# MoE, gates and final layer norm on 28 tiles of 128 tokens instead of 32 batches of 112

## Time and profile before

| what | value |
|---|---|
| median of 3 runs | 868.14 us (867.99 to 869.48) |
| the profiled execution's own time | 868.0 us |
| its span, first to last instruction | 866.2 us |
| PE busy | 829.0 us (96%) |
| DVE busy | 723.7 us (84%) |
| ACT busy | 650.5 us (75%) |

### The profile page before, as it was taken

One profiled execution on the slowest core, in us unless ns is written; L12 is line 12 of the kernel. 1 busy time (PEld: TensorE's weight loads), 2 busy tenths in 40 slices (PEclk: granted clock), 3 DMA queues, 4 the chain that ended last, 5 costly groups with the idle time before them and its releaser, 6 DMA issues.

```text
span 866.2 us, 25528 instructions
## 1 busy us (share of the span) xinstructions
PE 829.0 (96%) x7844; PEld 723.8 (84%) x7844; DVE 723.7 (84%) x2836; ACT 650.5 (75%) x1961; POOL 199.7 (23%) x293
## 2 busy tenths in 40 slices
PE   4789999999999999999999999999999999999985
PEld 3678888888888888888888888888888888888863
DVE  3547888888998888888988898998888998888765
ACT  2458877788887777888877788887777888777760
POOL 2202122222222222222222212222222222222101
PEclk9999999999999999999999999999999999999999
DMA  8634444443434444433444433444444333433300
GB/s 261 163 98 104 114 108 109 123 114 86 104 98 111 109 115 117 95 98 96 113 109 110 123 94 101 100 106 106 113 118 103 99 100 100 108 86 84 92 8 11
DMA packets 89830, 91.08 MB, mean 105 GB/s; under 512 B 19440, under 2 KB 85600, under 8 KB 89696
## 3 DMA queue, kind: packets, MB, share of 16 engines
q1 hardware_dynamic: 89696, 89.45, 41.0%
HBM read 26.84 MB, written 3.67 MB: 35 GB/s over the span
## 4 chain that ended last, share of the span: by engine, by line
PE 87%; DVE 3%; SPq 3%; DMA 2%; issue 2%; ACT 1%; POOL 1%; DVEq 0%; POOLq 0%; ACTq 0%
PE psum L1042 19%; PE psum L920 18%; PE psum L911 11%; PE psum L936 10%; PE psum L986 8%; PE psum L979 7%; PE psum L968 3%; PE psum L1000 3%; SPq L386 2%; SPq L395 1%; PE psum L957 1%; DVE mix L609 1%; PE psum L950 1%; PE psum L962 1%; DMA wout_sb<-in_wout 1%
## 5 line engine op out<-in xcount | busy, mean ns | idle before, releaser
L475 ACT ACTIVATE probs<-masked,nmax 112x375 f32<-112x375 f32 x512 | 312.9, 611 | 77.6 <-DVE nmax L595 76.6
L595 DVE CUSTOM_DVE_ANT_0 masked<-psum,mask_add 112x375 f32<-112x375 f32 x512 | 276.6, 541 | 53.7 <-PE psum L911 42.8
L505 ACT ACTIVATE probsT<-psum 125x336 f32<-125x336 f32 x512 | 228.6, 447 | 63.2 <-PE psum L920 58.3
L920 PE MATMUL psum<-const_sb,probs 112*125 112x112 f32 x1536 | 251.1, 272 | 0.1
L920 PEld LDWEIGHTS psum<-const_sb,probs 112*125 112x125 f32 x1536 | 235.8, 188 | 16.0 <-issue 6.8
L911 PE MATMUL psum<-k_stack,q_stack 96*112 96x376 f32 x512 | 203.4, 397 | 3.3 <-DMA k_stack<-k_hi 2.7
L418 POOL TENSOR_SCALAR var_eps<-moments 112x1 f32<-112x1 f32 x96 | 21.2, 220 | 485.6 <-DVE moments L699 191.1
L609 DVE SCALAR_TENSOR_TENSOR mix<-psum,gate,mix 112x256 f32<-112x256 f32 x224 | 107.7, 481 | 14.6 <-PE psum L1042 1.3
L1042 PE MATMUL psum<-we_hi,x_hi 128*112 128x512 f32 x256 | 108.0, 422 | 2.4 <-DVE mix L609 2.4
L911 PEld LDWEIGHTS psum<-k_stack,q_stack 96*112 96x112 f32 x512 | 90.1, 176 | 22.5 <-issue 13.4
L1042 PE MATMUL psum<-we_hi,x_lo 128*112 128x512 f32 x256 | 100.8, 394 | 0.0
(11 more groups left out here) (110 smaller groups left out, 1438.2 us busy)
## 6 DMA issues: line engine op xcount, KB each, us to landing
k_stack<-k_hi SPq DMA_DIRECT2D x256, 93.8 KB, 2.2
q_stack<-q_hi SPq DMA_DIRECT2D x256, 56.0 KB, 2.0
ctx_sb<-in_context_T SPq DMA_DIRECT2D x32, 376.0 KB, 3.3
k_stack<-k_lo SPq DMA_DIRECT2D x128, 93.8 KB, 2.2
q_stack<-q_lo SPq DMA_DIRECT2D x128, 56.0 KB, 2.0
xT<-in_x_T SPq DMA_DIRECT2D x32, 112.0 KB, 2.2
x_sb<-in_x SPq DMA_DIRECT2D x32, 112.0 KB, 2.2
out_dram<-out_sb SPq DMA_DIRECT2D x32, 112.0 KB, 1.9
```

The lines of the kernel that those rows point to most:

```text
L475: nc.scalar.activation(probs[:, n % RING, :], masked[:, n % RING, :], ACT.Exp, bias=nmax[:, n:n + 1], scale=-1.0, accum_out=probs_sum[a[1] ...
L505: nc.scalar.activation(probsT[:, i % TRING, :], psum[0:KP, T_BANKS[i % 2], 0:KT * TOK], ACT.Copy).then_inc(probsT_copied, 1)
L595: nc.vector.tensor_tensor_reduce(masked[:, n % RING, :], psum[0:TOK, S_BANKS[n % 2], 0:KEYS], mask_add[k][:, :], 1.0, 3.0e38, ALU.add, ALU ...
L920: mm = nc.tensor.transpose(psum[0:KP, T_BANKS[n % 2], j * TOK:(j + 1) * TOK], probs[:, n % RING, j * KP:(j + 1) * KP], ident[0:TOK, 0:TOK])
```

## The change

Logits, gate, MoE, third layer norm and store work on tiles of 128 token rows that cross batches. Seven tiles fill eight batches, so these stages run for batches with `batch % 8 > 0`: the gate (now a stage of its own, `gate`) rests in iterations 1, 9, 17 and 25, and `moe` in iterations 2, 10, 18 and 26. `x2_hi` and `x2_lo` become rings of 8 batches = 7 tiles. `x2` itself is written per batch as before and then moved by two new transfers on SP, behind the `k_stack` transfers, into one of two tiles `x2_tile` [128 x 256]: the head (the rows that complete the present tile) and the tail (the rows that begin the next one). `expert(0)` waits for both.

```diff
+def active(stage, it):
+    batch = it + STAGES[stage][0]
+    if stage in ("gate", "moe"):
+        return 0 <= batch < BATCH and batch % GROUP > 0
+    return 0 <= batch < BATCH
+
+def tile_of(at):
+    t, b = at
+    return t, b - 1 - b // GROUP
...
-        wk_sb, wv_sb = sb("wk_sb", [128, DC, DIM]), sb("wv_sb", [128, DC, DIM])
...
+        probsT_all = sb("probsT", [128, TRING, KT * TOK])
+        probsT = probsT_all[0:KP, :, :]
+        staging = probsT_all[:, :, :].rearrange("p t n -> p (t n)")
+        wk_sb, wv_sb = [staging[:, n * DC * DIM:(n + 1) * DC * DIM].rearrange("p (c n) -> p c n", c=DC) for n in range(2)]
...
+        x2_tile = [sb(f"x2_tile{k}", [ROWS, DIM]) for k in range(2)]
+        x2_hi = sb("x2_hi", [128, DC, RING_TOKENS], f32r)
+        x2_lo = sb("x2_lo", [128, DC, RING_TOKENS], f32r)
...
@@ SP: store
-                    sp.dma_start(out[row(shift(m, -1))], out_sb[1 - k][:, :]).then_inc(out_written[1 - k], 16)
+                    sp.dma_start(out_rows[row(done) * ROWS:(row(done) + 1) * ROWS, :], out_sb[done[1] % 2][:, :])\
+                      .then_inc(out_written[done[1] % 2], 16)
...
@@ SP: behind the k_stack transfers
+                if join:
+                    b = row(o) % GROUP
+                    sp.wait_ge(dve_join.sem, dve_join.to("x2", o))
+                    settle(sp)
+                    if gated:
+                        sp.dma_start(x2_tile[g[1] % 2][ROWS - STEP * b:ROWS, :], x2[1 - k][0:STEP * b, :])\
+                          .then_inc(x2_head_moved[g[1] % 2], 16)
+                    if b < GROUP - 1:
+                        if due(dve_moe.to("e0", shift(g, -1))):
+                            sp.wait_ge(dve_moe.sem, dve_moe.to("e0", shift(g, -1)))
+                            settle(sp)
+                        sp.dma_start(x2_tile[1 - g[1] % 2][0:TOK - STEP * b, :], x2[1 - k][STEP * b:TOK, :])\
+                          .then_inc(x2_tail_moved[1 - g[1] % 2], 16)
...
@@ DVE: expert(0)
-                        dve.wait_ge(dve_join.sem, dve_join.to("gate", m))
+                        dve.wait_ge(dve_gate.sem, dve_gate.to("gate", m))
+                        dve.wait_ge(x2_head_moved[m[1] % 2], turn(m, 1))
+                        dve.wait_ge(x2_tail_moved[m[1] % 2], turn(m, 1))
...
@@ DVE: x2, slot 9
+                            before = shift(o, -2)
+                            if row(before) >= 0 and active("gate", row(before) + 1):
+                                whole = tile_of(before)
+                                dve.wait_ge(x2_head_moved[whole[1] % 2], turn(whole, 1))
+                            if row(before) >= 0 and row(before) % GROUP < GROUP - 1:
+                                begun = shift(tile_of(before), 1)
+                                dve.wait_ge(x2_tail_moved[begun[1] % 2], turn(begun, 1))
...
@@ PE: lg and m0 to m3
-                        hi, lo = (x2_hi[1 - k], x2_lo[1 - k]) if name == "lg" else (x2_hi[k], x2_lo[k])
+                        tile = row(g if name == "lg" else m) % RING_TILES
+                        hi, lo = [half[:, :, tile * ROWS:(tile + 1) * ROWS] for half in (x2_hi, x2_lo)]
...
-                                mm = nc.tensor.matmul(bank[0:TOK, 0:width], x_part[:, c, :], w_part[:, c, :],
+                                mm = nc.tensor.matmul(bank[:, 0:width], x_part[:, c, :], w_part[:, c, :],
```

More of the change, by code:

```diff
@@ L262, in decoder_layer @@
         pe_steps = {stage: Chain(sem(f"pe_{stage}"), [u for u, _, _ in ALL_USES if STAGE_OF[u] == stage])
-                    for stage in ("self", "proj", "join", "moe", "weights")}
+                    for stage in ("self", "proj", "join", "gate", "moe", "weights")}
         act_steps = {stage: Chain(sem(f"act_{stage}"), names) for stage, names in (
@@ L266, in decoder_layer @@
             ("proj", ["x1T", "q0", "q1", "k_hi0", "k_hi1"]),
-            ("join", ["o_sb", "x2_hi", "gate_exp"]),
+            ("join", ["o_sb", "x2_hi"]),
+            ("gate", ["gate_exp"]),
             ("weights", [f"we_hi{j}" for j in range(EXPERTS_PER)]))}
@@ L306, in stages, with ring, finished @@
         def stages(it):
-            return [active(stage, it) for stage in ("self", "proj", "attn", "join", "moe")]
+            return [active(stage, it) for stage in ("self", "proj", "attn", "join", "gate", "moe")]
         def batches(at):
-            return *[shift(at, ahead) for ahead in (2, 1, 0, -1, -2)], at[1] % 2
+            s, p, a, o, m = [shift(at, ahead) for ahead in (2, 1, 0, -1, -2)]
+            return s, p, a, o, tile_of(o), tile_of(m), at[1] % 2
+        def ring(batch):
+            b = row(batch) % GROUP
+            return slice(b * TOK, (b + 1) * TOK)
+        def finished(at):
+            return tile_of(shift(at, -3))
         block = ctx.enter_context(nc.Block())
@@ L352, in iteration @@
             def iteration(at, it):
-                own, proj, attn, join, moe = stages(it)
-                s, p, a, o, m, k = batches(at)
+                own, proj, attn, join, gated, moe = stages(it)
+                s, p, a, o, g, m, k = batches(at)
                 if active("self", it + 1):
@@ L384, in iteration @@
                     for n in range(PAIRS):
-                        for g, part in enumerate((q_hi, q_hi, q_lo)):
-                            sp.dma_start(q_stack[1 - k][32 * g:32 * g + 32, :, n, :, :].bitcast(fp32),
+                        for third, part in enumerate((q_hi, q_hi, q_lo)):
+                            sp.dma_start(q_stack[1 - k][32 * third:32 * third + 32, :, n, :, :].bitcast(fp32),
                                          part[32 * n:32 * n + 32, :, :, :].bitcast(fp32))\
```

188 lines of the change are left out of this document (100 added, 88 removed).

## The result

| | before | after |
|---|---|---|
| median of 8 runs | 868.57 us (867.57 to 871.23) | 863.82 us (860.08 to 868.74) |
| the profiled execution | 868.0 us | 860.08 us |
| its span | 866.2 us | 858.3 us |

The ratio is 0.9945, with a 95% interval of 0.9919 to 0.997. The sign and the profiled execution are near the forecast (858.1 us); the median is 5.7 us above it and outside the range. Two things want an explanation: what is missing in the profile, and why the median lies 3.7 us above the profiled execution. The runs of the changed kernel also spread over 8.7 us, those of before over 3.7.

What follows compares the result with a forecast made beforehand. PE was taken to bound full iterations (24.96 us) and the SP queue those without `moe`; -11.2 - 1.2 + 2.4 = -10.0 us took the median of 868.14 to 858.1 us, range 852.5 to 863.5.

Steps and rivals of the forecast that it cites:

- The short iterations: Four iterations without `moe`, ended by the SP queue's stack transfers: 2.8 us saved each, 11.2 us in all.
- worst bound: SP issues its 24 transfers in 17.48 us, as in a full iteration: 1.5 us saved each, 6.0 us in all.
- signs of being wrong: Full iterations longer than 25.1 us, or iterations without `moe` under 20 us or over 23.5 us.
- The gates: Logit matmuls on PE absent in iterations 9, 17 and 25: 0.39 us each, 1.2 us saved.
- Wider stationary operands: Loads of 128 instead of 112 columns in 28 iterations: 1.6 us for logits, 0.8 for expert blocks, 2.4 us cost.
- rival 4: Weight loads of exactly 128 columns take about half the time, turning the load cost into a gain: 850.2 us; chance 3%.
- 128 partitions: DVE, ACT and POOL instructions on 128 partitions instead of 112: no cost.
- the moves: Two more SP transfers behind the last `k_stack` transfer, some 1.2 us, hidden: nothing; uncovered 34 us.
- the new wait: `expert(0)` waits for the moved rows: 1.8 us of cover, 0.5 after an iteration without `moe`, so no cost.
- Rival 3: Moved rows land late and hold `expert(0)`: 1.5 us in 28 iterations, 42 us slower, 900 us; chance 3%.
- rival 1: PE alone bounds the iterations without `moe`: 20.6 and 1.6 us come off, 2.4 is paid, 848.3 us; chance 5%.
- rival 2: Iterations without `moe` only let ACT and DVE catch up: 869.3 us, in effect no change; chance 4%.

Runs made afterwards that it cites:

- V1 exchanged: Product V1 moved to slot 14 on bank G0, logits to slot 15 on G2: 863.8 us on the changed kernel, 869.57 us on the one before.
- first repeat: The changed kernel run again with nothing edited: 862.46 us, ratio 0.9938 to the kernel before.

## Why the prediction failed, step by step

**The short iterations: the step that failed, by its size (2.8 us a pair forecast, 1.4 measured).** The mechanism was right: the SP queue ends them. The term was mis-sized. The prediction set a short iteration and the one behind it against two full ones, 49.92 us, and took 2.8 us for each pair, 11.2 in all. In the profile the four pairs take 48.9, 48.9, 47.9 and 48.4 us, so they save 1.1, 1.0, 2.0 and 1.5: 5.6 in all, under even its worst bound of 6.0. (The table's 7.4 is against the same eight iterations of the kernel before, which took 201.5 and not 199.7 us, half of it because its iteration 2 was late from iteration 1, 25.86 us.)

From the second iteration's scores in slot 1 to the next such scores iterations 10, 18 and 26 take 23.73, 22.72 and 23.23 us, and iteration 1 took 22.00 in the kernel before. The prediction took this one iteration, in which SP issued its 24 transfers in 16.15 us, as the price of all. It wrote down the other end too (17.48 us, as in a full iteration) and called it the worst case; here the transfers take 17.03, 16.55 and 17.08 us, between the two. SP's timeline of iteration 10 shows the difference; it answers to the earlier trace rows:

```profile
295.13 1.71 SPq L425 DMA_DIRECT2D q_stack<-q_hi  x2
...
304.74 1.24 SPq L434 DMA_DIRECT2D k_stack<-k_hi  x2
306.03 1.64 SPq L434 DMA_DIRECT2D k_stack<-k_lo  x1
307.71 1.24 SPq L434 DMA_DIRECT2D k_stack<-k_hi  x2
...
311.56 0.60 SPq L434 DMA_DIRECT2D k_stack<-k_hi  x1
```

One transfer holds the queue for 0.60 us, two for 1.24. The first pair took 0.47 more than that, and the one at 306.03 a whole 1.04 more. Iteration 1 of the kernel before, where the prediction says "back to back", had one such stall too, a small one of 0.63 us:

```profile
85.19 1.23 SPq L395 DMA_DIRECT2D k_stack<-k_hi  x1
```

What single transfers took over 0.60 us comes to 0.63 us there, and to 1.47, 0.98 and 1.56 us in iterations 10, 18 and 26. That is 0.84, 0.35 and 0.93 more, and the 24 transfers took 0.88, 0.40 and 0.93 us longer than the 16.15, so the stalls account for nearly all of it.

On PE the same stretch of iteration 10 is a row of waits, the last of which is the one to compare with 93.25 in the earlier trace rows:

```profile
308.65 0.39 PE L975 MATMUL psum<-k_stack,q_stack 96*112 96x376 f32 x1 [0.86 <-issue]
...
310.00 0.40 PE L975 MATMUL psum<-k_stack,q_stack 96*112 96x376 f32 x1 [0.25 <-issue]
...
311.88 0.39 PE L975 MATMUL psum<-k_stack,q_stack 96*112 96x376 f32 x1 [0.43 <-issue]
```

The waits are named "issue" because the view names no releaser; the landings do. The last `k_stack` transfer that the scores at 311.88 need is issued at 309.64 and lands 2.1 us later, at 311.8; the one for the scores at 310.00 is the first of the two at 307.71, which stood behind the stall and lands 2.2 us later, at 309.9. The waits are gone when SP has only 20 transfers to issue. Beside each of these stalls lies an instruction fetch on a queue of its own. The DMA queues between 304.0 and 306.2 us (queue: packets, MB, share; then KB and median us to landing of the issues):

```profile
q8 instruction: 1, 0.02, 3.9%
k_stack<-k_hi SPq DMA_DIRECT2D x3, 93.8 KB, 3.5
k_stack<-k_lo SPq DMA_DIRECT2D x2, 93.8 KB, 2.7
```

and the next 4 us have none. There are 64 such packets in the span, one in 13.4 us. In iteration 1 of the kernel before one came while SP was waiting, at 74 us, and the next at 84.75, beside the stall shown above. In the whole profile of the changed kernel 54 of the 768 stack transfers held SP for over 0.9 us, and 53 of them have such a fetch beside them. That fetch and stall come together is what the traces show; that the one causes the other is argued, since no run took the fetches away. The rest of the shortfall in these iterations lies between the slot 1 scores and the first stack transfer: 6.98, 6.42 and 6.42 us, where iteration 1 had 6.10 and a full iteration 6.93. The prediction had this part as 0.8 us of gain; it is 0 to 0.5.

None of the prediction's signs of being wrong came up: the full iterations' median stayed under 25.1 us, and the short ones, 22.0 to 23.4, between 20 and 23.5. A sign for a size has to stand as close as the range does.

**The gates: -1.2 forecast, 0 measured.** The stretch from slot 12 to slot 15 isn't PE's. It ends with `expert(5)` emptying V1's bank, so the logits lie in a gap (iterations 9, 17 and 25 take 25.02 us, the others 25.04). Iteration 9 of the changed kernel, which has no gate, shows the gap that they had covered:

```profile
282.35 0.38 PE L1050 MATMUL psum<-wv_hi,ctx_hi 128*125 128x256 f32 x1 [0.25 <-DVE mix L665]
```

The error was to read a PE without idle time in the earlier trace rows as a PE that is the bound at every place. Ends of matmuls are modelled, and a wait shorter than the overlap leaves no idle time.

**Wider stationary operands: +2.4 forecast, about +1.6 by the median full iteration** (25.04 against 24.96, 20 times), and +0.5 in the sum over all, as some full iterations before were longer than the median. The spacing of the logit matmuls was right, about 112 ns:

```profile
256.49 0.26 PE L1095 MATMUL psum<-wr_parts,x_hi 128*128 128x16 f32 x1
256.61 0.25 PE L1098 MATMUL psum<-wr_parts,x_lo 128*128 128x8 f32 x1
256.72 0.26 PE L1095 MATMUL psum<-wr_parts,x_hi 128*128 128x16 f32 x1
```

But these are the same gap-hidden matmuls as above, so the 1.6 us laid on them weren't paid there, and what carries the 0.08 us an iteration in this order of products is not shown. With V1 exchanged, where the logits do count, the two kernels are 0.05 us apart (24.91 and 24.86), about what four logit matmuls at 14 ns more come to. The loads themselves answer to the earlier trace rows, 175 ns there:

```profile
L1107 PEld LDWEIGHTS psum<-we_hi,x_lo 128*128 128x128 f32 x224 | 42.9, 192 | 10.5
```

The mean grew by 17 ns for 16 columns, so rival 4, a quick load of 128 columns, is out for this type. The 13 ns that the prediction estimated from the Trainium skill ("TensorE: Matmul & The Clock Gate", section on LDWEIGHTS) were near; of the whole load the same rule makes an estimated 107 ns at 128 columns, which fits the spacing of 112 ns but not the 192 ns of this row.

**128 partitions, the moves, the new wait: nothing, as forecast.** In the tight case behind a short iteration SP issues the head's move at 312.28 and the tail's, which the next tile needs, at 312.96; a head of 16 KB lands in 1.8 us, at 314.1, and `expert(0)` starts at 315.08 without a wait. That is 1.0 us of cover, and behind the other three short iterations it is 0.8 to 0.9; the prediction had 0.5.

```profile
312.28 0.56 SPq L443 DMA_DIRECT2D x_tile<-x  x1
312.96 0.56 SPq L450 DMA_DIRECT2D x_tile<-x  x1
```

```profile
315.08 0.48 DVE L665 SCALAR_TENSOR_TENSOR mix<-psum,gate,x_tile 128x256 f32<-128x256 f32 x1
```

Rival 3 (moves late) is out by the run without the moves, rival 1 (PE alone) by the waits above, rival 2 (all given back) by the body's 7.0 us.

**What no step had: the granted clock.** The prediction took 1.00 for granted, as the earlier trace rows show it. Of the five profiles of the unedited changed kernel two have a body of 716.1 to 716.2 us and three, with a fall of the clock in iteration 2 or 11, of 718.9 to 720.7. Their mean is 718.3, which is 4.9 below the 723.1 before: the measured difference of the medians (4.75). The exchange on the changed kernel has the fall as well; none of the four profiles of the kernel before and of those built on it has it there. The profiled execution was thus a lucky one, its nearness to the forecast included, and the median pays 2 us more in the body. Two iterations without experts one behind the other (1 and 2) are where it happens most; before, only iteration 1 was short. In the tail such falls are seen in kernels built on the one before as well (two of the three profiles). The profile that goes with the result caught one there: the windows that hold the last tiles' experts, before and after, have a clock of 1.00 and 0.72.

```profile
830.00:848.00 18.00, 13.95 (x139) 10.80 (x138) 11.36 (x44) 8.23 (x25) 1.58 (x4) 1.00 0.03 8
```

```profile
831.80:849.80 18.00, 13.53 (x42) 10.19 (x42) 9.62 (x32) 0.75 (x3) 1.80 (x5) 0.72 0.07 21
```

What stays open is why the clock falls in one execution and not in the next: the profile that goes with the result had a wait of 1.08 us in the same place and its first repeat one of 1.30, and neither had a fall.

## What to carry to other kernels

Taking work from the busiest engine pays only down to the next bound, and that bound should be priced from several iterations: an issuing queue without slack pays for stalls of up to 1 us each, and the one iteration that the price came from had only 0.6 us of them. Where an engine with modelled ends shows no idle time, look for a producer that ends within 0.1 us of its next step (here the emptying of a PSUM bank) before counting a saving there. Work that is taken out in lumps leaves PE waiting, and the granted clock may fall behind the wait. In the one profile with matmuls put into the gaps it didn't; thinning the work evenly was not tried.

## What the runs showed of the hardware that was not expected

- Queue issue of one stack transfer takes SP 0.60 us, and now and then 1.6, with a 16 KB instruction fetch beside it (53 of 54 times in the changed kernel's profile); the `k_stack` transfers issued around the stall of iteration 10 land after 2.7 to 3.5 us in the median instead of 2.2.
- Six `k_stack` transfers issued by POOL take it 0.53 to 0.64 us each and land after 2.8 us, and the kernel's full iterations grow by 0.56 us, with V1 waiting for DVE, whose busy time grows by 1.2 us. Four issued by ACT hold it some 0.62 us each.
- In four of the seven profiles whose iteration 2 starts with a wait of 1.1 to 1.3 us on a PE that otherwise worked, the granted clock fell to half for 3 to 7 us, at a cost of 2.7 to 4.5 us in the unedited ones. In the five where the waits there are 0.62 us or less, one of them with matmuls put into the waits, it did not.
